# Hybrid attention block on one core: the second batch's projections placed between the first step's maxima

## What is computed

```
q, k, v = y @ Wq + bq, y @ Wk + bk, y @ Wv + bv      # y = x, normalised over its 256 features
scores  = q @ k^T / 4                                # per batch and head, 2048 x 2048
out     = softmax(scores) @ v
x       = x + out @ Wo + bo
```

## Time and profile before

| | us |
|---|---|
| median of 3 runs (2261.27 to 2267.18) | 2264.39 |
| the profiled execution, its own time | 2264.34 |
| its span | 2262.3 |
| PE busy | 2097.6 (93%) |
| DVE busy | 1836.0 (81%) |
| ACT busy | 1412.4 (62%) |
| POOL busy | 116.3 (5%) |
| PE's first score product of step 0 that adds the maxima (L575) | at 216.46 |

### The profile page before, as it was taken

How to read it: one execution, slowest core, us unless ns; L and a number is a source line. 1 busy time by engine, 2 the same in 40 slices (tenths; PEclk the granted TensorE clock), 3 DMA queues, 4 the chain that set the end, 5 groups by cost and what they waited for, 6 DMA issues and landing times.

```text
span 2262.3 us, 47874 instructions
## 1 busy us (share of the span) xinstructions
PE 2097.6 (93%) x14214; PEld 868.4 (38%) x14214; DVE 1836.0 (81%) x3464; ACT 1412.4 (62%) x2787; POOL 116.3 (5%) x174
## 2 busy tenths in 40 slices
PE   3559999999999999999999999988996899997997
PEld 2331333333333333333333333244433555554433
DVE  3239999999999999999999999744549577777366
ACT  2330888888888888888888888844442344333443
POOL 1111000000000000000000000010002000002000
PEclk8775999999999999999999999999996999998998
DMA  5132112122121221212212121130000000000002
GB/s 140 45 93 73 41 42 73 46 59 59 43 72 43 63 56 46 73 40 65 53 49 70 40 69 50 53 117 25 1 0 1 1 0 1 1 0 0 1 0 75
DMA packets 93620, 100.64 MB, mean 44 GB/s; under 512 B 35713, under 2 KB 74897, under 8 KB 93553
## 3 DMA queue, kind: packets, MB, share of 16 engines
q1 hardware_dynamic: 93552, 99.79, 15.9%
HBM read 78.72 MB, written 20.71 MB: 44 GB/s over the span
## 4 chain that ended last, share of the span: by engine, by line
PE 84%; DVE 8%; issue 3%; ACT 2%; DMA 1%; SPq 1%; POOL 0%; DVEq 0%; POOLq 0%; ACTq 0%
PE ps L546 22%; PE ps L520 14%; PE ps L569 10%; PE ps L575 10%; PE ps L652 8%; PE ps L660 4%; PE ps L733 2%; PE ps L491 2%; PE ps L742 2%; DVE mx L1149 2%; PE ps L477 2%; PE ps L762 1%; PE ps L535 1%; PE ps L673 1%; PE ps L667 1%
## 5 line engine op out<-in xcount | busy, mean ns | idle before, releaser
L1149 DVE TENSOR_REDUCE mx<-ps 128x1 f32<-128x512 f32 x2048 | 1277.1, 683 | 6.5 <-PE ps L520 2.8
L895 ACT ACTIVATE YT<-ps 128x512 f32<-128x512 f32 x2048 | 1057.8, 606 | 294.4 <-PE ps L575 294.3
L546 PE MATMUL ps<-YT,work 128*32 128x512 f32 x4096 | 546.3, 606 | 0.0
L520 PE MATMUL ps<-work 64*128 64x512 bf16 x2048 | 475.1, 394 | 11.6 <-DVE mx L1149 7.4
L569 PE MATMUL ps<-work 64*128 64x512 bf16 x2048 | 395.6, 378 | 0.3
L575 PE MATMUL ps<-work 34*128 34x512 bf16 x2048 | 394.7, 378 | 0.0
L520 PEld LDWEIGHTS ps<-work 64*128 64x128 bf16 x2048 | 146.6, 93 | 627.3 <-DVE mx L1149 553.1
L569 PEld LDWEIGHTS ps<-work 64*128 64x128 bf16 x2048 | 162.6, 95 | 93.0 <-ACT YT L895 17.5
L652 PE MATMUL ps<-YT,c_s 128*128 128x512 f32 x384 | 177.4, 605 | 2.5 <-ACT work L935 2.5
L477 PE MATMUL ps<-ident,xn 128*128 128x128 f32 x256 | 53.2, 368 | 100.8 <-DVE xn L1063 92.5
L935 ACT ACTIVATE work<-ps,bias 128x512 f32<-128x512 f32 x96 | 60.7, 683 | 126.7 <-PE ps L652 126.7
(11 more groups left out here) (126 smaller groups left out, 1635.7 us busy)
## 6 DMA issues: line engine op xcount, KB each, us to landing
work<-k_scr SPq DMA_DIRECT2D x640, 64.0 KB, 2.1
work<-q_scr SPq DMA_DIRECT2D x640, 32.0 KB, 1.8
o_scr<-o_sb SPq DMA_DIRECT2D x32, 256.0 KB, 2.1
q_scr<-work SPq DMA_DIRECT2D x48, 128.0 KB
X<-in_L_attn_a_x_dram SPq DMA_DIRECT2D x8, 512.0 KB, 8.3
work<-negt SPq DMA_DIRECT2D x256, 1.0 KB
work<-o_scr SPq DMA_DIRECT2D x16, 256.0 KB
work<-inv_scr SPq DMA_DIRECT2D x16, 256.0 KB
```

The source lines that it names most:

```text
L520: mm(ps[:, bank_of[x], :], qa[rows, p, jp, qt * P:(qt + 1) * P], ka[rows, p, kc_ * CH:(kc_ + 1) * CH], start=True, stop=True).then_inc(a_m ...
L546: m = mm(ps[32 * j:32 * j + 32, 7, :], vst[:, p, t, :], prob[:, (GROUP * t + j) % 8, :], start=t == 0, stop=t == KTILES - 1)
L895: fn(prob[:, u % 8, :], ps[:, S_BANK + u % S_RING, :], ACT.Exp, scale=HD ** -0.5).then_inc(exp_ok, 1)
L1149: dve.tensor_reduce(mx[:, p, at_:at_ + 1], ps[:, bank_of[x], :], AX_X, ALU.max).then_inc(a_max, 1)
```

## The change

**Loads and norms.** The second chunk of `x` is loaded before the first weights; the output bias `bo_s` moves to the later weights. DVE scales chunks 0 and 1 at once and then runs two chunks ahead of the projections; its moments of all eight chunks are done in the loop over the first four.

**First batch (chunks 0 to 3).** PE projects tile by tile (`project_heads`), each with its own semaphore count, so that ACT can begin at the first. `low` is done by POOL. The coarse loads of step 0 are issued before chunk 3's low part is stored.

**Second batch (chunks 4 to 7).** Its tiles are projected into banks 3 to 5, its values into bank 6, its transposes into bank 7, between the first step's maxima. Its `residue` and `low` are done by POOL, its parts lie in `qkf_b` and `part_b`, one buffer to a part. `scaled` of chunks 6 and 7 and `put_values` of 4 to 7 stand between DVE's maxima. POOL's bias adds come last. `prob` now takes 4 tiles in each half of `YT`, the first batch's columns.

The diff, cut to its core:

```diff
+        def stored(eng, pt, c):
+
+            if c >= 0:
+                eng.wait_ge(p_st[pt][c % 2], STORED * (c // 2 + 1))
...
-                if c == 0:
+                if c == 1:
...
+                store(c, 0, p_act)
+                store(c, 1, p_mid)
                 if c == CPG - 1:
-                    for p in range(2):
-                        sp.wait_ge(p_st[p], 16 * STORED * (c + 1) // 2)
-                    for s in (0, 1):
-                        load_coarse(qa, ka, s, s, qa_ld)
-            for p in range(2):
-                sp.wait_ge(p_st[p], 16 * STORED * NCH // 2)
+                    for pt in range(2):
+                        stored(sp, pt, c - 1)
+                        stored(sp, pt, c)
+                    load_coarse(qa, ka, 0, 0, qa_ld)
+                store(c, 2, p_low)
+                if c == CPG - 1:
+                    load_coarse(qa, ka, 1, 1, qa_ld)
+                    stored(sp, 2, c - 1)
+                    stored(sp, 2, c)
+                    load_scores(0, 0)
+                if c == CPG:
+                    load_scores(1, 1)
+            for pt in range(3):
+                for c in (NCH - 2, NCH - 1):
+                    stored(sp, pt, c)
...
-            for s in (0, 1):
-                load_scores(s, s)
             sp.wait_ge(nm_t, 1)
             load_negated(0)
             refill_max(0, 0)
...
+            def project_heads(c, n):
+
+                if n == 0:
+                    pe.wait_ge(n_y, 2 * (c + 1))
+                if c == CPG:
+                    pe.wait_ge(p_val, c)
+                wait(pe, p_act, 3 * (c - 1) + n + 1)
+                for kt in range(KT):
+                    w = wq_s[:, kt, n * P:(n + 1) * P] if n < KT else wkk_s[:, kt, :]
+                    m = mm(ps[:, qk_bank(c, n), :], w, YT[:, kt, ch(c)], start=kt == 0, stop=kt == KT - 1)
+                m.then_inc(p_mm, 1)
+
+            def project_values(c):
                 wait(pe, p_val, c)
...
+            turn_chunk(0, 0)
+            turn_chunk(0, 1)
+            pe.wait_ge(w0_ld, 16 * len(first_weights))
+            for c in range(CPG):
+                for n in range(3):
+                    project_heads(c, n)
+                project_values(c)
+                if c + 2 <= CPG:
+                    turn_chunk(0, c + 2)
...
+            def first_maxima(*those):
+                for x in those:
+                    max_mm(0, 0, x)
+
+            pe.wait_ge(p_act, 3 * CPG)
+            for c in range(CPG, NCH):
+                x = BLOCK * (c - CPG)
+                first_maxima(*range(x, x + 4))
+                project_heads(c, 0)
+                first_maxima(*range(x + 4, x + 8))
+                project_heads(c, 1)
+                if c + 1 < NCH:
+                    pe.wait_ge(n_xn, c + 2)
+                    turn_rows(0, c + 1, 0)
+                first_maxima(*range(x + 8, x + 12))
+                project_heads(c, 2)
+                if c + 1 < NCH:
+                    turn_rows(0, c + 1, 1)
+                first_maxima(*range(x + 12, x + 14))
+                project_values(c)
+                first_maxima(*range(x + 14, x + 16))
             for x in range(AHEAD):
                 max_mm(0, 1, x)
+            pe.wait_ge(n_y, 2 * NCH)
+            pe.wait_ge(p_act, 3 * NCH)
+            pe.wait_ge(p_val, NCH)
             pe.wait_ge(kb_ones, 2)
...
+            def high(c, n):
+
+                act.wait_ge(p_mm, 4 * c + n + 1)
+                if n == 0:
+                    if c not in (CPG, CPG + 1):
+                        wait(act, p_low, c - 1)
+                    if c > CPG:
+                        act.wait_ge(p_res, c)
+                        stored(act, 0, c - 1)
+                    elif c < CPG:
+                        stored(act, 0, c - 2)
+                b = bias[:, BQ + n:BQ + n + 1]
+                fn(qkf(c)[:, n, :], ps[:, qk_bank(c, n), :], ACT.Identity, bias=b)
+                fn(part(c, 0)[:, n, :], ps[:, qk_bank(c, n), :], ACT.Identity, bias=b).then_inc(p_act, 1)
...
+                if c > CPG:
+                    act.wait_ge(p_low, c)
+                    stored(act, 1, c - 1)
+                elif c < CPG:
+                    stored(act, 1, c - 2)
+                act.copy(part(c, 1), qkf(c)).then_inc(p_mid, 1)
...
+            for c in range(CPG, NCH):
+                high(c, 0)
+                high(c, 1)
+                if c + 1 < NCH:
+                    put_row(0, c + 1, 0)
+                high(c, 2)
+                if c + 1 < NCH:
+                    put_row(0, c + 1, 1)
+                middle(c)
+            for pt in range(3):
+                for c in (NCH - 2, NCH - 1):
+                    stored(act, pt, c)
...
+            for c in range(2):
+                dve.wait_ge(x_ld[c], 16)
+                moments_of(0, c)
+                scaled(0, c)
+            dve.wait_ge(x_ld[2], 16)
+            moments_of(0, 2)
+            dve.wait_ge(w0_ld, 16 * len(first_weights))
+            for c in range(CPG):
+                scaled(0, c + 2)
+                residue(c)
+                put_values(c)
+                for ahead in (2 * c + 3, 2 * c + 4):
+                    if ahead < NCH:
+                        dve.wait_ge(x_ld[ahead], 16)
+                        moments_of(0, ahead)
...
+                    if not before and x % BLOCK == 3 and CPG + 2 + x // BLOCK < NCH:
+                        scaled(0, CPG + 2 + x // BLOCK)
+                    if not before and x % BLOCK == BLOCK - 1:
+                        put_values(CPG + x // BLOCK)
...
+            def residue(c):
+                pool.wait_ge(p_act, 3 * (c + 1))
+                pool.tensor_tensor(qkf(c), qkf(c), part(c, 0), ALU.subtract).then_inc(p_res, 1)
+
+            def low(c):
+                pool.wait_ge(p_mid, c + 1)
+                if c != CPG:
+                    stored(pool, 2, c - 1 if c > CPG else c - 2)
+                pool.tensor_tensor(part(c, 2), qkf(c), part(c, 1), ALU.subtract).then_inc(p_low, 1)
+
...
+            for c in range(CPG):
+                for ahead in (2 * c + 3, 2 * c + 4):
+                    if ahead < NCH:
+                        root(0, ahead)
+                low(c)
+
+            for pt in range(3):
+                for c in (CPG - 2, CPG - 1):
+                    stored(pool, pt, c)
+            pool.wait_ge(p_low, CPG)
...
+            for c in range(CPG, NCH):
+                residue(c)
+                low(c)
+            pool.wait_ge(w_ld, 16 * len(weights))
+            for c in range(NCH):
+                add_bias(c)
+            pool.wait_ge(p_val, NCH)
+            pool.wait_ge(n_bo, NCH)
```

More of the change, by code:

```diff
@@ L848, in _, with put_row @@
             fn = act.activation
+            def put_row(st, c, kt):
+                act.wait_ge(n_t, 2 * (st * NCH + c) + kt + 1)
+                act.copy(YT[:, kt, ch(c)], ps[:, turn_bank(st, c, kt), :]).then_inc(n_y, 1)
             def put_rows(st, c):
                 for kt in range(KT):
-                    act.wait_ge(n_t, 2 * (st * NCH + c) + kt + 1)
-                    act.copy(YT[:, kt, ch(c)], ps[:, turn_bank(st, c, kt), :]).then_inc(n_y, 1)
-            def high(c):
-                p = c % 2
-                act.wait_ge(p_mm, c + 1)
-                wait(act, p_low, c - 1)
-                wait(act, p_st[p], 16 * STORED * (c // 2))
-                for n in range(3):
-                    b = bias[:, BQ + n:BQ + n + 1]
-                    fn(qkf[:, p, n, :], ps[:, n, :], ACT.Identity, bias=b)
-                    m = fn(part[:, p, 0, n, :], ps[:, n, :], ACT.Identity, bias=b)
-                m.then_inc(p_act, 1)
+                    put_row(st, c, kt)
@@ L867, in middle @@
             def middle(c):
                 act.wait_ge(p_res, c + 1)
-                act.copy(part[:, c % 2, 1], qkf[:, c % 2]).then_inc(p_mid, 1)
-            for c in range(NCH + 2):
-                if c < NCH:
-                    put_rows(0, c)
-                if c == 0:
-                    act.wait_ge(w0_ld, 16 * len(first_weights))
-                if 1 <= c <= NCH:
-                    high(c - 1)
-                if c >= 2:
-                    middle(c - 2)
+                if c > CPG:
[3 more added lines that the diff above has]
+                    stored(act, 1, c - 2)
@@ new lines, in middle @@
+                act.copy(part(c, 1), qkf(c)).then_inc(p_mid, 1)
+            put_rows(0, 0)
+            put_rows(0, 1)
+            act.wait_ge(w0_ld, 16 * len(first_weights))
+            for c in range(CPG):
+                for n in range(3):
+                    high(c, n)
+                if c + 2 <= CPG:
+                    put_rows(0, c + 2)
+                middle(c)
[7 more added lines that the diff above has]
+                    put_row(0, c + 1, 1)
+                middle(c)
@@ L894, in step @@
                             wait(act, pv_mm, KTILES * s + t - 1)
[L895 removed]
```

(4 more changed lines are left out.)

140 lines of the change are left out of this document (57 added, 83 removed).

## The result

The changed kernel takes 2225.87 us (median of 4 runs, 2219.72 to 2231.01) against 2264.97 us for the kernel before (4 runs beside it): a ratio of 0.9826, 95% interval 0.9808 to 0.9843. It gains 39 us. The prediction said 2197.0 us, 67 us of gain, with a range from 2184 to 2217: the direction was right, the time lies 9 us above the range. It happens to be the 2225 us of rival (c), whose mechanism did not occur, as will be seen.

A forecast was written before the change was run, and what follows sets the result against it. PE fills the steps, so the gain comes from the start: first maxima at 69 us, last head tile at 128, tail 21.3, step 0's maxima at 149.3, 67 earlier. 2264.3 minus 67 gives 2197 us, range 2184 to 2217.

The forecast's parts named there:

- rival (c): Second batch: a POOL subtraction stops all DVE reductions, eight of 3.5 us adding 28, giving 2225 us; chance 4%.
- [N]o instruction of the steps changes but the place of `prob`, so I expect nothing there: Steps, 224 to 1460 us: PE is busy throughout at full clock, so no change in time.
- everything behind it as before: Sign of a right forecast: after the first L619 product at about 149 us, nothing changes.
- rival (d): Steps: tiles in the far half of `prob`, 8 KB apart, are slower; at 3 us a step 2293 us; chance 3%.
- steps longer than 39 us: Sign that rival (d) holds; the steps were taken as about 39 us each.
- Edits at nothing: Before chunk 4's `residue`: POOL's ones rows (7 us) and copies (1.2) end at 80, ahead of need, costing nothing.
- First batch done by about 51: Chunks 0 to 3: PE needs 8.7 us a chunk at full clock, from about 17 us on.
- First maxima at 69: Start of maxima, after SP's late stores and loads: 69 us in place of 168, bounds 66 and 71.
- Last head tile of chunk 7 at 128, 59 us after the first product: Maxima with chunks 4 to 7 between them: blocks of 14.2 us, 58 to 59 us in all.
- Rival (a): Maxima with second batch: PE clock stays low, 38 us more if always, taken as +19, 2216 us; chance 18%.
- Rival (b): Second batch: one buffer a part keeps chunks in single file, 20 us each, +18, 2215 us; chance 10%.
- The tail, 21.3 with POOL's subtraction at 3.5: Behind the last head tile: conversion, subtractions, store, landing and negated maxima in line; step 0 gets its maxima at 149.3.

The follow-up runs named there:

- experiment 2: The changed kernel with 80 redundant waits ahead of ScalarE's step 0, putting its loop 40 instructions later: 2210.31 us, ratio 0.9767.
- Experiments 4 and 5: Changed kernel with chunk 6's scaling issued before the first maxima: 2216.91 us; the same plus 80 redundant waits ahead of ScalarE's step 0: 2203.05 us.
- experiment 6: The kernel of experiment 2 with POOL's two memsets of the ones rows issued twice: 2216.07 us, ratio 0.9788.
- Experiment 7: Changed kernel with early chunk 6 scaling, 80 ScalarE waits and 15 extra unread matmuls before the first maxima: 2197.84 us; with 90 matmuls: 2263.63 us.
- experiment 8: The kernel of experiment 2 with the second batch projected straight after the first and all 64 maxima behind it: 2225.53 us, ratio 0.983.

## Why the prediction was wrong

What gives the gain was right: the projections do hide between the maxima, and the first L619 comes 52.6 of the 67 us earlier. Two steps failed; each put at nothing what was a loss.

**"[N]o instruction of the steps changes but the place of `prob`, so I expect nothing there", and "everything behind it as before".** This is the larger one, and no rival covered it: rival (d) looked for a loss in the steps, but in the data's place and not the code's. ScalarE's loop had moved by 9 instructions and was fetched again at each turn, 14.3 us in the trace, 15.6 by experiment 2. (The prediction also took a step for 39 us, dividing by one step too many; it is 40.16 in the kernel before, so that "steps longer than 39 us" as a sign of rival (d) would have held there too.) Ahead of the result nothing in the trace of before showed that its place was a lucky one, but that the number of ScalarE's instructions ahead of the loop changed could have been counted.

**"Edits at nothing. The ones rows (7 us) and copies of POOL (1.2) ... end at 80".** POOL's own durations were right (3.50, 3.54 and 1.23 us; it begins at 75.0, late with the store, and ends at 83.4), and nothing waited for POOL. But their neighbour on DVE was not looked at. In the kernel before these memsets ran beside reductions from PSUM alone; the change put a scaling there, and it paid 7.1 us (8.36 less 1.28). Experiments 4 and 5 get 9.0 and 7.3 us of the kernel's time back; experiment 6, with twice the memsets, makes the scalings longer still. Rival (c) asked the right question, but only of the reductions, and these indeed keep their 0.6 us beside POOL. The scaling is another case: it may run in a two-port mode (one that also uses the pair of SBUF ports which DVE shares with POOL), and then by the Trainium skill's "SBUF — State Buffer", section "Who interferes with whom", the holder of the pair blocks the other engine for a whole instruction. The trace agrees with that blocking, one scaling to a memset; whether the scalings do run in such a mode, no run here shows. DVE's subtractions, with two SBUF inputs, pay beside POOL's as well. Chunk 1's, beside a subtraction on POOL from 32.23 to 35.33, takes 3.93 us, chunk 2's, alone, 1.76:

```profile
33.01 3.93 DVE L1182 TENSOR_TENSOR work<-work 128x1536 f32<-128x1536 f32 x1 [0.97 <-ACT work L938]
...
45.35 1.76 DVE L1182 TENSOR_TENSOR work<-work 128x1536 f32<-128x1536 f32 x1 [3.38 <-ACT work L938]
```

The other terms, one by one:

- *First batch done by about 51.* Right: the last values end at 50.3.
- *First maxima at 69.* 72.17. SP's chain went nearly as drawn (first store 37.22, eleven parts issued by 59.31 instead of 57.4), but the landing took 3.74 us and not the 2.4 taken. The bound of 71, with 3.3 for each landing, was a better guide; it is passed by one.
- *Last head tile of chunk 7 at 128, 59 us after the first product.* 143.9, after 71.7: 12.7 too many. The memsets are up to 7 of them, and chunk 7's scaling was held 2.0 us beside POOL's `low` (3.29 at 99.63 instead of 1.28). At full clock a block takes 14.9 us (from chunk 6's second head tile at 123.65 to chunk 7's at 138.51), where 14.2 were drawn. The rest is clock: in this execution the low level came back at about 99 to 109 and 116 to 123, and a head tile took 3.78.
- *Rival (a), low clock.* It held in part: the mean over the stretch is 0.79, not 0.50. This is what the Trainium skill's "TensorE: Matmul & The Clock Gate", section "A second HAM failure mode: psum-queue depth-cycling", warned of. Its price isn't settled. Experiment 7 gets 5.2 us back, not 19; and the three kernels with the same code here come to their first L619 8 us apart, in the order of their clocks.
- *Rival (b), chunks in single file.* Didn't happen here, but experiment 8 shows the file with its real waits once the maxima no longer cover them.
- *The tail, 21.3 with POOL's subtraction at 3.5.* 19.9; the subtraction takes 3.09.
- *Sum.* 67 less 3.2 (start) and 12.7 (maxima and chunks), plus 1.4 (tail), is 52.5, the 52.6 measured; less 14.3 in the steps is 38. With the three losses that could be removed gone, the kernel takes 2197.84 us. That it is the figure of the prediction is in part chance: the late start of 3 us is still in it, and the extra matmuls are not in the change.

## What to carry to other kernels

When a change adds or removes instructions ahead of a loop, even waits alone, count how many, for each engine with a long loop. (Here only ScalarE's was moved and tried.) If the steps of a loop get longer without any of their instructions having changed, look at the packets of the instruction queue first, and shift the loop before you look for anything else. And if a helper's work on POOL is "hidden", ask not only who waits for it, but what DVE runs beside it now: its neighbour may be another than before.

## What was not expected of the hardware

- The place of ScalarE's loop of 294 instructions in its program is worth 0.5 to 1.1 us a turn of 80.3 us: 13 jumps back, 14.3 us, 0.6% of the kernel. 9 redundant instructions ahead of it cost the kernel before 17 us (2280.07 against 2262.73; 15.6 by the ratio), 40 bring the changed kernel 15.6 (13 by the ratios).
- Four scalings of 128x256 float32 by DVE beside two memsets of 2x4096 bf16 by POOL take 8.36 us instead of 1.28, beside four of them 14.20. The memset reads nothing. A negation of 128x16 with two SBUF inputs (L1227) takes 3.03 us beside a 3.09 us subtraction of POOL (from 149.96); reductions from PSUM beside the same are not touched.

```profile
150.04 3.03 DVE L1227 SCALAR_TENSOR_TENSOR negq<-mxq,negq 128x16 bf16<-128x16 f32 x1
```

- 15 matmuls whose results nobody reads, in a wait of 22 us, make the kernel 5.2 us faster. They don't keep the clock high: the first head tile behind them is at the low level again (3.68 us), the next at the upper (1.98); without them the low level lasts longer (mean clock from 72 to 90 us 0.69, with them 0.91).
